# Cross-attention with a routed FFN: bodies of the attention loop rearranged, prologue work moved into body 0

## What is computed

```python
q_in = x @ Wq + _lora(x, q_down, q_up, q_alpha)
k_in = org_ctx @ Wk + _lora(org_ctx, k_down, k_up, k_alpha)
v_in = org_ctx @ Wv + _lora(org_ctx, v_down, v_up, v_alpha)
out = _attention(q_in, k_in, v_in) + IPA_SCALE * _attention(q_in, ipa_ctx @ Wk_ipa, ipa_ctx @ Wv_ipa)
return out @ Wo + bo + _lora(out, o_down, o_up, o_alpha)
...
x = x + _L0_xattn_ref(_layernorm(x, axis=-1), ctx_768, ...)
x = x + _L0_ffn_ref(_layernorm(x, axis=-1), gate_w, w1, w2)   # top 2 of 8, softmax weights, silu
```

## Times and profile before

| what | us |
|---|---|
| runs before, median of 3 (lowest, highest) | 834.12 (829.76, 836.23) |
| the profiled execution's own time | 830.35 |
| its span, first to last instruction | 828.6 |
| TensorE busy | 695.4 (84%) |
| VectorE, ScalarE, GpSimd busy | 528.4, 449.2, 494.1 |
| mean granted TensorE clock | 0.963 |

### The profile page before, as it was taken

How to read it: one execution, slowest core, us unless ns; L and a number is a source line. 1 busy time by engine, 2 the same in 40 slices (tenths; PEclk the granted TensorE clock), 3 DMA queues, 4 the chain that set the end, 5 groups by cost and what they waited for, 6 DMA issues and landing times.

```text
span 828.6 us, 23021 instructions
## 1 busy us (share of the span) xinstructions
PE 695.4 (84%) x7980; PEld 580.9 (70%) x7981; DVE 528.4 (64%) x1226; ACT 449.2 (54%) x772; POOL 494.1 (60%) x584
## 2 busy tenths in 40 slices
PE   6757889799788789789799898864499999999994
PEld 2235777677677677677677776643398888888894
DVE  5955786686586586586586586573255555555552
ACT  1537775674675675675674675661244343443441
POOL 2227467667667667667668668666147555655565
PEclk9999999999999999999999999987599999999998
DMA  9901001101101101101101101101535556555450
GB/s 267 285 1 40 28 18 61 52 14 64 52 13 64 52 13 64 52 13 64 52 13 65 52 13 64 53 13 62 161 66 98 81 89 98 86 91 81 83 91 6
DMA packets 41676, 54.69 MB, mean 66 GB/s; under 512 B 6320, under 2 KB 36016, under 8 KB 41648
## 3 DMA queue, kind: packets, MB, share of 16 engines
q1 hardware_dynamic: 26176, 35.90, 14.8%
q0 software_dynamic: 14384, 17.33, 12.0%
q10 hardware_dynamic: 1088, 1.08, 0.4%
...
## 4 chain that ended last, share of the span: by engine, by line
PE 57%; ACT 14%; issue 13%; DVE 8%; DMA 2%; POOL 2%; SPq 1%; another core or an unknown queue 1%; POOLq 1%; ACTq 0%; DVEq 0%
PE ps L1321 46%; PE ps L1382 5%; ACT pt_s L873 4%; PE ps L1392 2%; ACT wstage L992 2%; ACT xn L935 2%; PE ps L439 2%; DVE ot_s L1073 2%; DMA out_x<-pt_s,token_of 1%; POOL out_x L413 1%; PE ps L1347 1%; ACT ot_s L873 1%; DVE picked L1227 1%; DVE prob L1114 1%; ACT row_words L944 1%
## 5 line engine op out<-in xcount | busy, mean ns | idle before, releaser
L413 POOL DMA_INDIRECT out_x<-pt_s,token_of x78 | 125.9, 1615 | 31.1 <-issue 30.2
L492 ACT ACTIVATE q_s<-ps 128x512 f32<-128x512 f32 x78 | 46.6, 597 | 132.6 <-PE ps L1321 132.1
L1321 PE MATMUL ps<-q_s,ffnw 128*128 128x256 f16 x936 | 110.0, 275 | 0.0
L1321 PE MATMUL ps<-ffnw,ot_s 128*128 x936 | 108.7, 273 | 0.1
L565 DVE TENSOR_TENSOR ot_s<-q_s,ot_s 128x512 f16<-128x512 f32 x78 | 54.0, 692 | 85.8 <-ACT ot_s L496 57.8
L1144 DVE TENSOR_REDUCE mx<-prob 128x16 f32<-128x1168 f32 x64 | 47.9, 790 | 95.3 <-ACT prob L913 90.9
L1321 PEld LDWEIGHTS ps<-ffnw,ot_s 128*128 128x128 f16 x936 | 90.2, 98 | 13.3 <-issue 1.9
L1321 PE MATMUL ps<-wo_s,ot_s 128*128 128x256 f16 x768 | 93.8, 281 | 5.4 <-DVE ot_s L1073 4.4
L1321 PEld LDWEIGHTS ps<-q_s,ffnw 128*128 x936 | 90.7, 99 | 10.7 <-issue 0.2
L731 POOL TENSOR_TENSOR prob<-prob,mx 128x1168 f32<-128x1168 f32 x64 | 77.6, 1235 | 31.0 <-DVE mx L1144 30.7
L1321 PE MATMUL ps<-xt_s,wq_s 128*128 128x256 f16 x768 | 89.0, 277 | 3.8 <-DVE xt_s L1073 1.9
...
## 6 DMA issues: line engine op xcount, KB each, us to landing
...
out_x<-x_sb SPq DMA_DIRECT2D x16, 256.0 KB, 2.2
out_x<-pt_s,token_of POOLq DMA_INDIRECT x78
...
```

Of the source, the lines that this page charges most:

```text
L413: pool.indirect_dma_start(out_rows, bass.IndirectOffsetOnAxis(ap=token_of[:, j % UNROLL, c:c + 1], axis=0), y_sb[:, j % UNROLL, c, :], Non ...
L492: act.activation(h32[:, half, :], h_ps(j, half), ACT.Silu, scale=1 / WSCALE).then_inc(silu_done, 1)
L1321: last = pe.matmul(o, lhs(a, n), rhs(c, n), start=(i == 0), stop=(i == len(steps) - 1))
```

## The change

In the prologue only the first quarter of x is loaded, and norm statistics are taken of six tiles (sequences 0 to 2, `LEAD`); the other three quarters are loaded after the ipa values are out, into space that till then stages the matrices vi, v and o (`x_stage`), and their statistics are taken two tiles per body in `residual` (`x_left`). The square root and reciprocal give way to a power on GpSimd. Each weight matrix has a staging buffer of its own. The lora additions and splits of v and o, and the ipa values with their way to `v_s`, move into body 0; GpSimd makes all three passes (scale, copy, subtract) over vi and wo itself, and the low parts of the context. In the bodies the scatters of b-2 come after the second `normalise` of body b, ScalarE's FFN copies (`fw_high`) between the two score copies, `normalise_x` before the head copies (`ot`), `row_high` and `gap_e` behind them, and VectorE's `place_rows` after the first of its four head splits. `x2n` gets a buffer of its own.

The diff, SP's queue, GpSimd and ScalarE:

```diff
-            load_job(4)
-            load_job(5)
+            sp.dma_start(wstage[:], ffn_w[0]).then_inc(fw_in, 16)
...
+            sp.wait_ge(w_split, 4)
+            load_x(1, x_rest)
+            sp.wait_ge(w_split_p, 1)
+            load_x(2, x_rest)
+            sp.wait_ge(w_split_p, 2)
+            load_x(3, x_rest)
...
             def body(b, first, last):
                 if not first:
                     sp.wait_ge(fw_split, b)
-                else:
-                    sp.wait_ge(ipa_split, 4)
-                sp.dma_start(wstage[:], ffn_w[b]).then_inc(fw_in, 16)
-                if not first:
+                    sp.dma_start(wstage[:], ffn_w[b]).then_inc(fw_in, 16)
...
+            pool.wait_ge(consts2, 14)
+            pool.wait_ge(ag1_done, 1)
+            pool.tensor_tensor(ln1_s[:, 0, :], ln1[:, :, 1], eps[:], ALU.add).then_inc(var1, 1)
...
+            def split_job(n):
+                done = POOL_JOBS.index(n) + 1
+                if jobs[n] in lora_jobs:
...
+                    last = pool.tensor_scalar(stage[n][0:rows, lo:hi], stage[n][0:rows, lo:hi], WSCALE, None, ALU.mult)
...
+                    last = pool.tensor_copy(dst_flat(jobs[n], 0)[0:rows, lo:hi], stage[n][0:rows, lo:hi])
...
+                    last = pool.tensor_tensor(dst_flat(jobs[n], 1)[0:rows, lo:hi], stage[n][0:rows, lo:hi],
                                               dst_flat(jobs[n], 0)[0:rows, lo:hi], ALU.subtract)
                 last.then_inc(w_split_p, 1)
-            pool.wait_ge(w_split_p, 3)
+
+            split_job(4)
+            pool.wait_ge(w_split, 2)
...
+            def body(b):
+                first, settled = isinstance(b, int) and b == 0, not (isinstance(b, int) and b < 2)
                 shift(b, 0)
                 shift(b, 1)
                 normalise(b, 0)
                 if not first:
                     rstd_2(b - 1)
                 normalise(b, 1)
+                if settled:
+                    scatter(b - 2)
+                if first:
+                    split_job(5)
+                pool.wait_ge(fw_hi, b + 1)
+                fw = [ffnw[:, part, bass.ds(b, 1), :].rearrange("p e n -> p (e n)") for part in (0, 1)]
+                pool.tensor_tensor(fw[1], wstage[:], fw[0], ALU.subtract).then_inc(fw_split, 1)
                 if not first:
-                    row_low(b - 1)
+                    router_gap(b - 1)
                 pool.wait_ge(xn_done, b + 1)
                 xb = x_sb[:, bass.ds(b * TPB, TPB), :]
                 pool.tensor_tensor(xb, xb, bo_sb[:].unsqueeze(1).to_broadcast([P, TPB, DM]), ALU.add
                                    ).then_inc(bo_added, 1)
                 if not first:
-                    router_gap(b - 1)
-                pool.wait_ge(fw_hi, b + 1)
-                fw = [ffnw[:, part, bass.ds(b, 1), :].rearrange("p e n -> p (e n)") for part in (0, 1)]
-                pool.tensor_tensor(fw[1], wstage[:], fw[0], ALU.subtract).then_inc(fw_split, 1)
-                if not first:
+                    row_low(b - 1)
                     weigh_picks(b - 1)
-                    scatter(b - 1)
-                    scatter_pick(1)
...
                 copy_scores(b, 0)
                 if not last:
                     xt(b + 1)
+                if first:
+                    split_job(3)
+                else:
+                    fw_high(b)
                 copy_scores(b, 1)
+                if first:
+                    fw_high(b)
                 exp(b, 0)
+                if first:
+                    normalise_lead(2)
                 if not last:
                     q(b + 1, 0)
                     q(b + 1, 1)
...
                     q(b + 1, 3)
                 v(b, 0)
                 if first:
+                    ipa_v_hi(act)
                     act.wait_ge(pt_zeroed, 1)
                 pt(b, 0)
                 pt(b, 1)
...
                 pt(b, 6)
                 pt(b, 7)
+                if x_left:
+                    normalise_x(b + 2, ln2_s[:, 1, TPB:2 * TPB], ln2_s[:, 2, TPB:2 * TPB])
+                for k in range(4):
+                    ot(b, k)
                 if not first:
                     row_high(b - 1)
+                    gap_e(b - 1)
+
+            def fw_high(b):
                 act.wait_ge(fw_in, 16 * b + 16)
                 act.activation(wstage[:], wstage[:], ACT.Copy, scale=WSCALE).then_inc(fw_scaled, 1)
                 act.wait_ge(fw_scaled, b + 1)
                 act.activation(ffnw[:, 0, bass.ds(b, 1), :].rearrange("p e n -> p (e n)"), wstage[:], ACT.Copy
                                ).then_inc(fw_hi, 1)
-                ot(b, 0)
-                ot(b, 1)
-                if not first:
-                    gap_e(b - 1)
-                if x_left:
-                    act.wait_ge(row_lo, b + 1)
-                    normalise_x(b + 2)
-                ot(b, 2)
-                ot(b, 3)
-
-            split_job(0)
-            split_job(1)
...
+            split_job(0)
+            act.wait_ge(rstd1, 1)
+            normalise_lead(0)
+            ctx_hi(0)
             xt(0)
+            split_job(1)
+            ctx_hi(1)
             q(0, 0)
             q(0, 1)
+            split_job(2)
             q(0, 2)
             q(0, 3)
-            split_job(5)
             act.wait_ge(zeroed, 1)
             k_(0, 0)
             k_(0, 1)
             ipa_k_hi(act)
-            ipa_v_hi(act)
-            act.wait_ge(ipa_split, 4)
+            act.wait_ge(ipa_split, 2)
             put_kipa(0)
-            normalise_x(1)
-            body(0, True, False, True)
+            normalise_lead(1)
+            body(0, True, False, False)
             with act.Fori(1, BATCH - 2) as b:
                 body(b, False, False, True)
```

VectorE:

```diff
+                if x_left:
+                    dve.wait_ge(x_rest, 48)
+                    for t in range(TPB):
+                        tile = (b + 3) * TPB + t
+                        dve.bn_stats(st2[:, TPB + t, :], x_sb[:, bass.ds(tile, 1), :].rearrange("p t d -> p (t d)"))
...
                     picked[:], picks[:], place[:].unsqueeze(1).to_broadcast([P, TOPK, TPB, EXPERTS]), ALU.mult))
+                dve.wait_ge(scattered, 64 * b + 16)
                 with nc.allow_low_precision(reason="whole numbers below 2 ** 24"):
                     dve.tensor_reduce(slot_i[:].rearrange("p k t -> p (k t)"),
...
                 maxima(b, 0)
                 if not last:
                     xt(b + 1)
+                if first:
+                    job_add(5, 0)
                 maxima(b, 1)
+                if first:
+                    job_add(5, 1)
+                    job_lo(3, w_split)
                 sums(b, 0)
                 if not last:
                     q(b + 1, 0)
                 if not first:
-                    residual(b - 1)
+                    residual(b - 1, x_left)
                 if not last:
                     q(b + 1, 1)
+                if first:
+                    job_add(5, 2)
                 sums(b, 1)
                 if not last:
                     q(b + 1, 2)
                     q(b + 1, 3)
+                if first:
+                    job_add(5, 3)
                 v(b, 0)
+                if first:
+                    vipa_lo()
                 pt(b, 0)
                 pt(b, 1)
                 v(b, 1)
...
                 if not first:
                     chain = pick_experts(b - 1)
                 ot(b, 0)
-                ot(b, 1)
                 if not first:
                     place_rows(b - 1, chain)
-                ot(b, 2)
-                ot(b, 3)
+                for k in range(1, 4):
+                    ot(b, k)
+
+            def vipa_lo():
+                dve.wait_ge(ipa_hi, 2)
+                dve.scalar_tensor_tensor(
+                    out=vipa_s[:, 1, :], in0=ps[0:BATCH * IPA, 5:7, :].rearrange("p c n -> p (c n)"),
+                    scalar=1 / WSCALE, in1=vipa_s[:, 0, :], op0=ALU.mult, op1=ALU.subtract
+                ).then_inc(ipa_split, 2)
...
+                last = dve.bn_stats(st1[:, t, :], x_sb[:, t, :])
+            last.then_inc(st1_done, 1)
             scale_down(1)
-            job_adds(0)
+            dve.wait_ge(st1_done, 1)
+            for t in range(LEAD):
+                last = dve.bn_aggr(ln1[:, t, :], st1[:, t, :])
+            last.then_inc(ag1_done, 1)
+            job_lo(0, w_split)
+            for u in range(4):
+                job_add(1, u)
+            xt(0)
+            job_lo(1, w_split)
+            q(0, 0)
+            q(0, 1)
             scale_down(2)
-            job_lo(0)
-            job_adds(1, lambda u: bn(2 * u, 2))
-            scale_down(3)
-            job_lo(1)
-            for kk, rows in enumerate((P, CDR)):
-                lo_of(ctx_s[0:rows, 1, kk, :], cstage[kk][0:rows, 0:BATCH * CTX], 1.0, ctx_s[0:rows, 0, kk, :],
-                      c_hi, kk + 1, c_split)
-            job_adds(3, lambda u: bn(8 + 4 * u, 4))
-            job_lo(3)
```

(48 more changed lines are left out.)

306 lines of the change are left out of this document (139 added, 167 removed).

## The result

The changed kernel takes 843.67 us (median of four runs, 838.33 to 849.97), the kernel before 831.94 beside it: 1.015 times as long, 95% interval 1.010 to 1.020. The forecast was 782 and faster. It is slower, and by more than the 1% that was taken as measurable. The profiled execution is the fastest of the four: 838.33, span 836.5.

A forecast was written before the change was run, and what follows sets the result against it. Bounds: TensorE's slow instruction supply during scatters, ScalarE's unbroken work at the body's end, VectorE's prologue chain. Start -17, thirteen bodies -29, body 15 -5, after it +3: -48 from 830.35, so 782 us, range 765 to 802.

The forecast's parts named there:

- Prologue and body 0: Start of the kernel: shorter prologue, first scores at 43 us (-27), work moved into body 0 (+10), together -17 us.
- Step (1): Steady body: the scatters leave the second scores, where TensorE gets its instructions slowly; -2.5 us a body.
- the rival that a branch or the position makes this stall: The stall stays at the second scores whatever GpSimd does; a body takes 29.2 us, total 792 us, chance 0.15.
- Step (2): Steady body: FFN copies ahead of the second score copy cost at most 0.3 us, their load landing at about 3.1.
- In body 1: FFN weights queue behind 3 MB of x, which eats what the body would gain; difference 0.
- Step (3): End of a steady body: only normalise precedes ScalarE's head copies, next scores 1.9 us earlier; projection waits 0.2 longer.
- Step (4): Steady body: two more statistics and two aggregates on VectorE delay the values; between 0 and 1.0 us, taken as +0.7.
- Step (5): Steady body: scatters beside keys, transposes and router can bring the stall back there; 0 to 2.5 us, middle +1.3 taken.
- The rival that ended slower: slot_i waits for scatters of two bodies before; each body grows by excess landing time, 844 us at 7.5, chance 0.02.
- The rival of a worse new place with a late load: Stall of all of 2.5 us beside keys and transposes, FFN load late by 0.5; total 804 us, chance 0.1.
- body 15: Last body: no second round of queries, shorter end, scatters meet little work; -5 us.

## Why the prediction was wrong

**Prologue and body 0** (-17 forecast, -10.9). The mechanism held, both sizes were off. The rows of TensorE to compare with its steps (k products, queries, second keys, v products, first scores), and the last of GpSimd's passes over wo:

```profile
16.70 7.38 PE L1358 MATMUL ps<-ffnw 32*128 32x512 f32 x8 [5.18 <-DVE ffnw L1081]
...
26.63 7.14 PE L1345 MATMUL ps<-xt_s,wq_s 128*128 128x256 f16 x48 [1.50 <-DVE xt_s L1076]
...
37.31 1.66 PE L1345 MATMUL ps<-ctx_s,wk_s 128*128 128x73 f16 x24 [2.73 <-DVE q_s L1076]
...
41.04 4.69 PE L1358 MATMUL ps<-ffnw 32*128 32x512 f32 x8
...
45.66 1.74 PE L1402 MATMUL ps<-k_s,q_s 64*128 64x77 f16 x48
...
77.17 4.08 POOL L745 TENSOR_TENSOR wo_s<-x_sb,wo_s 128x2048 f16<-128x2048 f32 x1
```

The k products wait for VectorE's scaling and end at 24.1 instead of 22.2. The queries, begun at 26.63, end at 33.8 instead of 32.0, the second keys wait 2.73 for q_s behind VectorE's work on the ipa key weights, and the v products take 4.69 of the 3.6 to 7.1 allowed. First scores at 45.66 instead of 43. Body 0 takes 36.2 instead of 33. TensorE is busy for 32.1 of that at a mean clock of 0.79 (first scores 1.74 us), a term that the sum didn't have. But the passes over wo, which body 1 needs, are late as well: they end at 81.25, 35.6 after the first scores, where 27 to 32 was forecast, and 0.7 before body 1 begins. So the clock may not be the whole of it, and how much of the 3.2 is its share no run tells.

**Step (1), the scatters leave the second scores: -2.5.** Right, and shown alone in the kernel before. With it falls the rival that a branch or the position makes this stall: the loop is still there, and the second scores run in 1.03. The rule of the Trainium skill weighed in the prediction (Runtime: NRT & Kernel Launch, Instruction fetch mechanics) would have left the stall where it was, and the trace doesn't agree: 1.03 us for the 48 matmuls that took 3.56 in the earlier trace rows.

**Step (2), the FFN copies cost at most 0.3, "their load must land by 3.2, and is issued right after the v_s load, landing at about 3.1".** This step failed. The v_s load goes out at 0.26 us after the next scores' start, the FFN load at 1.06, and it takes 3.7 to land: 4.8. The condition was named, the landing put 1.7 too early. The cost is 1.4 us in each of 13 bodies, as the run with the early load shows. The kernel before could afford it, since there ScalarE reads this load 25 us into the body (305.38 - 280.03): moving the consumer forward had made the producer's place in SyncE's order matter.

**In body 1** I had written 0, since the load behind 3 MB of x "eats what it would gain". It eats more: VectorE idles 8.26 us ahead of the second maxima, and the body is 2.7 longer than before.

**Step (3), the end of the body: -1.9 + 0.2.** -1.6 measured. The picks, which I had left as before, ran into the bias addition, whose place moved from ahead of the router's gap to behind it; without that the end is another 0.84 shorter.

**Step (4), statistics on VectorE: +0.7.** 0.6 by the run that moves the two statistics (the two aggregates stayed).

**Step (5), the stall in the new place: +1.3, between 0 and 2.5.** This step failed most: 2.9 to 3.0, above its upper end. I had bounded it by the old price. In the old place the gaps shown are TensorE's, in a stream of matmuls; in the new one all three engines that work in turns there show them (the unnamed waits in the chain above), and the gaps add up along the chain. That this is why it is dearer is a reading of these rows; what the runs show is the price. The prediction named the denser demand, and then took the middle of the bounds instead of a value at their upper end. 1.6 to 1.7 us too little, times 13.

**The clock** was in no step of the bodies. The quiet body was compared with a quiet body, and in the changed kernel nearly every second body is not quiet. It explains little of the miss all the same: thirteen times the body shown are 414.8 us of 419.5, and in the kernel before 401.3 of 405.2, so 4.7 against 3.9.

**The rival that ended slower** (slot_i waiting for the scatters, 0.02) is not what happened: slot_i ends at 308.44, with the scatters issued by 301.48, and its chain runs through the picks. The rival of a worse new place with a late load, 804, was the right pair of mechanisms, at 0.1 and with too small a size for both. Its price was +1.2 and +0.5 a body on the forecast; it is +1.7 and +1.4. The chance of 0.02 for slower was set too low by the same step: both terms of this rival were capped by rows of another place.

Sum of the misses: 6.1 at the start, 2.7 in body 1, 13 x (1.4 + 1.7 + 0.1) = 42 and 1 to 2 of clock and rounding, 3.8 in body 15 (ScalarE waits 2.00 for its FFN load, and TensorE 2.02 for its picks), 0.2 behind it; 56 as measured.
